# Transposed attention scores in quarter-array matmuls instead of half-array ones, in a windowed attention and convolution kernel

## The reference, cut to what matters

```python
x = x + conv_ref(group_norm(x), ...)            # "L0": gated windowed attention
x = x + conv3x3(group_norm(x), W) + bias        # "L1"
# L0, for x of (2, 128, 128, 128):
g = clip((x * ac_w + ac_b) * x, 0, 6)
qkv = einsum('bchw,dc->bdhw', g, qkv_w)         # 16 heads of 8, windows of 8x8 = 64 tokens
attn = softmax(einsum('wnqd,wnkd->wnqk', q, k) * scale)
o = einsum('wnqk,wnkd->wnqd', attn, v)
out = einsum('bchw,dc->bdhw', o, proj_w) + proj_b
```

## Time and profile before

| | us |
|---|---|
| median of 3 runs | 1222.42 (1219.32 to 1224.76) |
| the profiled execution | 1213.3 |
| its span, first to last instruction | 1211.6 |
| mean granted TensorE clock | 0.952 of full speed |

### The profile page before, as it was taken

The page is one execution under the profiler, slowest core; times in us unless marked ns, Lnnn a source line. Parts: engine busy times, 40 slices in busy tenths (PEclk is TensorE's granted clock), DMA queues, the critical chain, the costliest instruction groups (busy, mean ns, idle before and its releaser), DMA issues.

```text
span 1211.6 us, 52709 instructions
## 1 busy us (share of the span) xinstructions
PE 1013.6 (84%) x23011; PEld 581.7 (48%) x23011; DVE 996.8 (82%) x1331; ACT 791.0 (65%) x1327; POOL 503.9 (42%) x469
## 2 busy tenths in 40 slices
PE   1059999999999984998862799999999999679996
PEld 1035655566556652443321555566666565334442
DVE  6857888898888763899996788889999886379996
ACT  1137877888878774555532588788888787546662
POOL 7013444555545433133342145454554544403335
PEclk9979999999999997999995799999999999879998
DMA  8054445444544430033352445444444444001112
GB/s 305 1 150 129 134 134 152 123 149 133 147 135 139 137 85 2 17 123 105 108 188 97 123 132 152 143 131 147 143 146 145 129 143 132 4 1 52 70 70 87
DMA packets 114917, 140.59 MB, mean 116 GB/s; under 512 B 25088, under 2 KB 91008, under 8 KB 113664
## 3 DMA queue, kind: packets, MB, share of 16 engines
q1 hardware_dynamic: 114688, 137.23, 36.2%
HBM read 67.96 MB, written 67.11 MB: 111 GB/s over the span
## 4 chain that ended last, share of the span: by engine, by line
PE 64%; DVE 19%; issue 8%; DMA 3%; ACT 2%; SPq 2%; POOL 2%; POOLq 0%; DVEq 0%; ACTq 0%
PE ps L907 12%; PE ps L888 11%; PE ps L915 9%; PE ps L876 8%; PE ps L984 5%; PE ps L845 5%; DVE work L756 5%; PE ps L846 5%; PE ps L847 5%; DVE work L752 4%; PE ps L863 4%; DVE st L602 1%; DVE work L734 1%; DVE st L805 1%; SPq L286 1%
## 5 line engine op out<-in xcount | busy, mean ns | idle before, releaser
L650 DVE TENSOR_REDUCE m_all<-ps 128x16 f32<-128x1024 f32 x256 | 313.5, 1225 | 102.0 <-PE ps L876 100.8
L367 POOL TENSOR_SCALAR work<-work 128x256 f32<-128x256 f32 x128 | 108.6, 848 | 389.4 <-DVE work L643 370.6
L845 PE MATMUL ps<-work,c_hi 128*128 128x512 f16 x384 | 148.5, 387 | 31.6 <-DVE work L756 31.6
L876 PEld LDWEIGHTS ps<-k_pl,q_bd 48*64 48x64 f16 x8192 | 90.0, 111 | 165.0 <-issue 121.0
L888 PE MATMUL ps<-q_bd,k_pl 128*64 128x256 f16 x2048 | 162.8, 281 | 6.8 <-ACT work L450 4.0
L450 ACT ACTIVATE late_probs<-ps,ws 128x1024 f32<-128x1024 f32 x128 | 142.8, 1115 | 37.8 <-PE ps L888 35.9
L876 PE MATMUL ps<-k_pl,q_bd 48*64 48x64 f16 x8192 | 118.6, 198 | 50.6 <-issue 34.6
L532 ACT CAST work<-work 128x512 f16<-128x512 f32 (+1 forms) x128 | 78.9, 622 | 117.7 <-DVE work L752 106.4
L450 ACT ACTIVATE work<-ps,ws 128x1024 f32<-128x1024 f32 x128 | 141.6, 1106 | 12.4 <-PE ps L888 10.5
L847 PE MATMUL ps<-work,c_hi 128*128 128x512 f16 x384 | 147.9, 385 | 0.0
L846 PE MATMUL ps<-work,c_lo 128*128 128x512 f16 x384 | 147.8, 385 | 0.0
(11 more groups left out here) (131 smaller groups left out, 1903.1 us busy)
## 6 DMA issues: line engine op xcount, KB each, us to landing
stack_scratch<-work SPq DMA_DIRECT2D x128, 256.0 KB, 2.4
q_bd<-stack_scratch SPq DMA_DIRECT2D x256, 96.0 KB
k_pl<-stack_scratch SPq DMA_DIRECT2D x128, 192.0 KB, 3.5
stack_scratch<-work SPq DMA_DIRECT2D x128, 128.0 KB, 2.6
out_dram<-work SPq DMA_DIRECT2D x32, 512.0 KB, 2.8
img<-in_x_dram SPq DMA_DIRECT2D x8, 1024.0 KB, 11.9
img<-in_x_dram SPq DMA_DIRECT2D x16, 512.0 KB, 4.3
q_bd<-m_pair SPq DMA_DIRECT2D x256, 8.0 KB
```

Of the source, the lines that this page charges most:

```text
L367: g.tensor_scalar(near[h], near[h], -2.0, None, ALU.add).then_inc(less_done, 1)
L650: v.tensor_reduce(m_all[:, 0, :, p], ps[:, S_B:S_B + 2, :].rearrange("p r (a k) -> p (r a) k", k=WIN), AX.X, ALU.max).then_inc(max_done, 1)
L845: t_.matmul(o, lhs_hi, rhs_hi, start=first, stop=False)
L876: mm = t_.matmul(ps[64 * w:64 * w + 64, S_B + r, at:at + WIN], q_bd[rows, md, r, g, j, tok], k_pl[rows, md, g, tok], start=True, stop=True)
```

## The change

`scores_t` makes 16 matmuls of 50 rows (the 48 rows of one r and the two rows of maxima), 64 weight columns and 128 moving columns (two j, 64 queries) in place of 8 of 128 rows and 256 moving columns. r now picks the half of the array's rows and the bank, c the half of its columns. `q_bd` loses its axis over r: the columns of both r share one place, in their own rows. The two banks now hold r = 0 and r = 1, each with both windows, in place of one window each; the exponential reads them with a rearranged pattern and writes `probs` with an order (w, r, ...), and the columns that `weigh` takes follow. The DMAs write as many bytes to as many partitions as before. `q_bd`'s clearing at the start is half as long.

```diff
-        q_bd = sb("q_bd", [P, BUFS, HR, HG, HJ, UT], F16)
+        q_bd = sb("q_bd", [P, BUFS, HG, HJ, UT], F16)
...
-                            sp.dma_start(q_bd[at:at + HROWS, md, r, :, j, :], q_rows[r, j]).then_inc(q_in, 16)
+                            sp.dma_start(q_bd[at:at + HROWS, md, :, j, :], q_rows[r, j]).then_inc(q_in, 16)
...
-                            sp.dma_start(q_bd[at:at + 1, md, r, :, :, :].rearrange("o g j (a t) -> o (g j a) t", a=PAIRS),
+                            sp.dma_start(q_bd[at:at + 1, md, :, :, :].rearrange("o g j (a t) -> o (g j a) t", a=PAIRS),
...
-            g.memset(q_bd[:, :, :, :, :, :].bitcast(F32), 0.0).then_inc(pool_set, 1)
+            g.memset(q_bd[:, :, :, :, :].bitcast(F32), 0.0).then_inc(pool_set, 1)
...
-                    a.activation(probs[h][:, p % 2, :], ps[:, ST_B:ST_B + 2, :].rearrange("p w t -> p (w t)"), ACT.Exp,
+                    a.activation(probs[h][:, p % 2, :].rearrange("p (w r t) -> p r w t", w=EACH, r=HR),
+                                 ps[:, ST_B:ST_B + 2, :].rearrange("p r (w t) -> p r w t", w=EACH), ACT.Exp,
                                  scale=ws[:, R_EXP:R_EXP + 1]).then_inc(exp_done, 1)
...
-                                                   q_bd[rows, md, r, g, j, tok], k_pl[rows, md, g, tok],
+                                                   q_bd[rows, md, g, j, tok], k_pl[rows, md, g, tok],
...
-                        for g in range(HG):
-                            a, c = g // 2, g % 2
-                            mm = t_.matmul(ps[64 * c:64 * c + 64, ST_B + w, a * 256:a * 256 + 256],
-                                           k_pl[:, md, g, tok], q_bd[:, md, :, g, :, tok],
-                                           start=True, stop=True)
+                        for a in range(HG // 2):
+                            for r in range(HR):
+                                rows = slice(64 * r, 64 * r + ROWS + 2)
+                                for c in range(2):
+                                    g, at = 2 * a + c, 256 * w + P * a
+                                    mm = t_.matmul(ps[64 * c:64 * c + 64, ST_B + r, at:at + P],
+                                                   k_pl[rows, md, g, tok], q_bd[rows, md, g, :, tok],
+                                                   start=True, stop=True)
...
-                    strips = [(2 * r + a, P * r + 256 * a) for r in range(HR) for a in range(2)]
+                    strips = [(2 * r + a, 256 * r + P * a) for r in range(HR) for a in range(2)]
```

## The result

The changed kernel takes 1242.69 us (median of 4 runs, 1241.22 to 1249.89) against 1221.22 us for the kernel before in the same comparison. The ratio is 1.0184, with a 95% interval of 1.0137 to 1.0231: 1.8% slower, where 1190 us had been forecast. The profiled execution takes 1242.2 us, 28.9 us more than the one before.

The account below looks back on a forecast made before the run. It took a two-iteration loop through the DMAs as the bound: period (13.0 + 9.6) / 2 = 11.3 us, saving 31 us plus 2 at stage ends, so 1222.4 - 33 = 1190 us; own range 1175 to 1208, overall 1155 to 1214.

Parts of the forecast that it names:

- The prices of the blocks: scores_t blocks on TensorE: 0.23 to 0.25 us each in place of 0.46, saving 0.84 us a unit.
- the drains at a change of shape: Between neighbouring scores and scores_t blocks: 0.09 us lost three times a unit, 0.28 us expected to go.
- The exponentials' new pattern: Exponentials on ACT, 1.11 us each, writing in runs of 256: 0 extra cost, at worst 0.1 us each.
- The rival that the quarters are issued one by one: scores_t matmuls on TensorE start 57 ns apart, a block lasts 0.91 us, the kernel slows to 1275 us; chance 0.05.
- the costs: Extra prices of the change, such as 2048 more matmuls and weight loads: 0 for their issue; exponentials and DMAs also 0.
- D: From m_lo done, through the maxima, query and key DMAs, to scores 0: falls from 13.7 to 13.0 us.
- E: From scores 0 to the next iteration's m_lo: falls from 9.9 to 9.6 us, with DVE and ACT almost late.
- the wait ahead of scores 0 larger, about 1 us: Sign of being right: TensorE waits about 1 us for keys and queries from DRAM, with a period near 11.3 us.
- The loop through the DMAs: Attention stages: D + E make two periods; period falls to 11.3 us, saving 0.51 us an iteration, 31 us over 60.
- The slower one: The rival that scores_t quarters are issued one by one on TensorE: 1275 us, chance 0.05.
- The way through DRAM gives it back: Rival: D grows to 13.9 us as reads and maxima crowd together, 1219 us, chance 0.08; milder form 1205 us, 0.10.
- more weight-load stalls inside the blocks: Sign of being wrong, on TensorE in the attention stages; no size given.

Follow-up runs that it names:

- count_only: The kernel before, each scores_t matmul cut in two of 128 columns, still 128 rows: as many matmuls as the changed kernel; 1251.8 us, ratio 1.024.
- before_s16: The kernel before with 16 scores matmuls of 128 columns in place of 32 of 64, first head's maxima standing in for the second's; 1198.37 us, ratio 0.980.
- after_s16: The changed kernel with 16 scores matmuls of 128 columns in place of 32 of 64, first head's maxima standing in for the second's; 1215.54 us, ratio 0.9942.
- before_s16_m2: before_s16 with two DMAs for the maxima in place of four; 1180.59 us, ratio 0.9672.
- after_s16_m2: after_s16 with two DMAs for the maxima in place of four; 1159.56 us, ratio 0.9496.
- after_m2: The changed kernel, all instructions kept, with two DMAs for the maxima in place of four; 1219.09 us, ratio 1.0011.
- fetch_alone: None of the kernel's work: 2048 short matmuls in quarters of the array without waits, first with no data moving, then again beside 512 KB copies; 267.24 us in all.

## Why the prediction was wrong, by its own steps

**What was right.** The prices of the blocks held. The 16 matmuls of `scores_t` start within 0.20 us; the next block begins 0.35 us after the first ahead of `weigh` (307.06 to 307.41; forecast 0.33), 0.24 us ahead of scores (302.49 to 302.73; forecast 0.25), and from scores to `scores_t` it is 0.27 us (304.53 to 304.80; forecast 0.29, before 0.38). On the drains at a change of shape, the rule of the Trainium skill (TensorEngine Tiling (Array Packing), section Key Properties) that changing the tile, unlike changing the mode, doesn't drain TensorE is borne out for 48 rows beside 50: no 0.09 us is left between these blocks. The floor of about 25 ns from start to start that the Trainium skill gives (TensorE: Matmul & The Clock Gate, section "Wait — 56ns, not 53.3ns?") doesn't hold for matmuls in different quarters: 16 start in 0.20 us, 13 ns apart. The exponentials' new pattern costs nothing (1113 and 1107 ns; before). The rival that the quarters are issued one by one was rightly held unlikely.

**The step that failed first** is in the costs: "PE gets 2048 matmuls and weight loads more ... so 0 for their issue". I compared densities within one block (32 in 0.26 us) and took that as the rate at which instructions can be had. A block can be dense for a moment; over an iteration the rate was 256 per 4.2 to 4.5 us, and the kernel before was, by the estimate above, within 0.5 us of that bound: 2.69 pieces x 4.2 = 11.3 us against a pace of 11.81. The runs show the price: the same number of instructions more, with blocks only 0.01 us longer, cost 28 us (`count_only`), and from before to after the gaps inside blocks grow from 8 to 48 us in 700. The traces of before had it in view: 182 pieces of instructions on q8, and 12 gaps inside blocks, which I put down to nothing. Its share of 1.1% of the DMA engines' time says nothing, since it is a chain of latencies, one piece after another.

**The second** is the term D, "D falls from its present mean ... to the DMAs' own 13.0", a mean of two rounds of which one had been worked out and not seen. Here are D and E of the forecast, means of 60 rounds from the timelines (us):

| | D | E | half the sum |
|---|---|---|---|
| forecast, after | 13.0 | 9.6 | 11.3 |
| before | 13.56 | 10.04 | 11.80 |
| after | 14.03 | 10.71 | 12.37 |
| `before_s16` | 13.38 | 9.83 | 11.60 |
| `after_s16` | 14.18 | 9.93 | 12.05 |
| `before_s16_m2` | 12.39 | 10.11 | 11.25 |
| `after_s16_m2` | 12.10 | 9.95 | 11.02 |

In the kernel after both grew, by 0.5 and 0.7 us. With the supply eased, the median of E is 9.58 us, as forecast, but D rose by 0.8 us where it should have fallen: it is the longer wait ahead of scores 0. Why keys and queries come later in some rounds no run shows. With two DMAs fewer D is 12.1.

**The third** is what the forecast named as a mere sign, "the wait ahead of scores 0 larger, about 1 us". It priced a wait at its own length. The runs show that of 19 waits of 2 us and more in one piece 13 stand in iterations with a stretch at 1.2 GHz, which costs 1.9 us on top of the wait (`after_s16`). The clock's dips were in the profile of before (0.952, and two iterations of 62, the first of each stage), and I asked of none what came before it.

**The loop through the DMAs** (D + E = two periods) holds as a sum in every kernel, since it is how D and E are defined; what it was worth is that shortening D alone gave 24 us on the kernel before. But of the 33 us forecast none arrived.

**The rivals.** The slower one had the right sign but another mechanism: matmuls issued one by one, +54 us. "The way through DRAM gives it back" put the loss in D, and D did grow by 0.5 us; but with all instructions kept, easing D (`after_m2`) still leaves the change 23 us slower, so the supply comes first. Neither is what came. The forecast's own line, "more weight-load stalls inside the blocks", as a sign of being wrong, is what came true, and D, at 14.0, lies off the 12.4 to 13.5 that it gave as another.

## What to carry to other kernels

Where one engine issues many short instructions, count them: the pieces on the instruction queue, times the time of one (here 256 instructions per 3.5 us alone, 4.2 us in company), is a bound beside busy time, and gaps marked "issue" inside a block with no wait are its sign. An edit that trades array columns for more instructions loses when that bound is near; make instructions larger first. And a wait in front of TensorE that grows from 1 to 3 us in one piece can cost more than itself (here 1.9 us more, in most of such cases); before an edit that speeds TensorE up ahead of such a wait is judged, shorten what it waits for.

## What the runs showed of the hardware that I had not expected

- TensorE's instructions come in pieces of 16 KB, 256 instructions, one per 3.45 to 3.73 us with no other transfer running (`fetch_alone`), and one per about 4.2 us in the attention stages. 2048 matmuls that each take 64 columns needed 55.6 us.
- Copies running beside it at 151 GB/s hardly slowed the supply (57.3 us for the second set).
- In `fetch_alone`, where TensorE stands still for 1.5 to 1.8 us after each 1.9 us of work, the matmuls last 238 ns in the median throughout, where the same shape has a median of 193 ns in the kernel before. That looks like the lower level, but the granted clock reads 1.00 there, so it stays open.
- After 2.67 us of standing still ahead of scores 0, the granted clock was 0.52 over the next 7 us, though TensorE was busy for 6.35 of them.
- Matmuls of no use ahead of a wait (0.75 us an iteration) paid off by 10 us in all.
- A DVE instruction of 0.82 us took 4.40 us while POOL cleared buffers at the kernel's start.

What stays open: why one piece takes 4.2 us on average in the attention stages (3.4 at the least) and 3.5 alone, when the copies of `fetch_alone` hardly slowed it; the kinds of transfers differ (small packets there, 512 KB here), and that was not tried apart. Why D grows with the change is open too. Nor does a run tell how the loss of after splits between its causes but for the sorting above.
